# Chunked retention on one core: key moves, states and table loads in another order, and k ahead of q in its array

## What is computed

```python
x = hidden_states                       # (2, 512, 512)
xn = layernorm(x)
qkv = silu(xn @ qkv_w.T)                # 32 heads of 128: q, k, v
# retention, per head h with its own decay, carried over blocks of the sequence:
#   out = (q k^T * diag_decay) v + (q * q_decay) state
#   state = state * block_decay + (k * k_decay)^T v
attn = attn * rsqrt(mean(attn ** 2) + eps)          # over all heads
att_out = sigmoid(xn @ gate_w.T) * (norm_w * attn) @ out_w.T
# eight LoRA experts of rank 16, the two best of each token, and a base layer
ffn = xn @ W_base.T + b_base + expert_out
out = x + att_out + ffn
```

## Time and profile before

| | |
|---|---|
| three runs | 1157.47, 1155.29, 1155.59 us; median 1155.59 |
| the profiled execution | 1158.24 us |
| its span in the profile | 1156.4 us |
| TensorE busy | 1083.6 us, 94% of the span |
| ScalarE, VectorE, GpSimd busy | 59%, 57%, 55% |
| TensorE's granted clock, mean | 0.973 |
| share of TensorE in the chain that ended last | 66% |

### The profile page before, as it was taken

One profiled execution on the slowest core, in us unless ns is written; L12 is line 12 of the kernel. 1 busy time (PEld: TensorE's weight loads), 2 busy tenths in 40 slices (PEclk: granted clock), 3 DMA queues, 4 the chain that ended last, 5 costly groups with the idle time before them and its releaser, 6 DMA issues.

```text
span 1156.4 us, 20519 instructions
## 1 busy us (share of the span) xinstructions
PE 1083.6 (94%) x6258; PEld 948.4 (82%) x6258; DVE 655.3 (57%) x1212; ACT 679.7 (59%) x1465; POOL 634.0 (55%) x626
## 2 busy tenths in 40 slices
PE   9998999899998999989998999989999899989988
PEld 8987879788897878978897888978789688977777
DVE  6865564656554574655645555545646557454547
ACT  9665555565565565665656655555656556556521
POOL 6557463564635645475626746356464655357444
PEclk9998999999998999999999999989999999999899
DMA  8223122232213221131221312132211322223232
GB/s 301 56 60 101 43 64 56 56 83 51 60 46 97 65 69 51 33 90 54 68 55 55 82 47 59 49 86 73 68 56 32 86 59 68 55 56 82 62 89 89
DMA packets 150690, 81.28 MB, mean 70 GB/s; under 512 B 108896, under 2 KB 130656, under 8 KB 150624
## 3 DMA queue, kind: packets, MB, share of 16 engines
q1 hardware_dynamic: 150336, 80.04, 25.2%
q10 hardware_dynamic: 288, 0.52, 0.1%
HBM read 65.32 MB, written 15.20 MB: 70 GB/s over the span
## 4 chain that ended last, share of the span: by engine, by line
PE 66%; DMA 8%; DVE 8%; ACT 7%; issue 6%; SPq 4%; POOL 1%; ACTq 0%; DVEq 0%; POOLq 0%
PE bank_q L1907 6%; PE bank_q L1909 6%; PE bank_q L1908 6%; PE bank_p L1907 4%; PE bank_p L1908 4%; PE outp L1907 4%; PE bank_p L1909 4%; PE outp L1908 4%; PE outp L1909 4%; PE bank_r L1907 4%; DMA keys_t<-keys_dram 4%; PE bank_r L1908 4%; PE bank_r L1909 4%; DMA keys_dram<-k_blocks 3%; PE att L2007 2%
## 5 line engine op out<-in xcount | busy, mean ns | idle before, releaser
L459 POOL TENSOR_TENSOR w_lo<-combo,w_hi 128x768 fp32r<-128x768 f32 (+1 forms) x128 | 164.9, 1293 | 142.8 <-ACT w_hi L655 142.1
L459 POOL TENSOR_TENSOR w_lo<-raw,w_hi 128x256 fp32r<-128x256 f32 (+1 forms) x128 | 132.8, 1040 | 120.5 <-ACT w_hi L655 120.0
L510 POOL TENSOR_TENSOR sum_sq<-sum_sq,square 128x512 f32<-128x512 f32 x64 | 82.6, 1291 | 117.7 <-ACT square L825 117.7
L1471 DVE TENSOR_TENSOR acc<-acc,outp 128x512 f32<-128x512 f32 x116 | 79.3, 684 | 61.7 <-PE outp L1909 61.2
L1907 PE MATMUL outp<-wo_hi,g_hi 128*128 128x512 f32 x250 | 100.2, 401 | 13.4 <-DVE g_lo L1417 8.2
L1908 PE MATMUL bank_q<-c_lo,w_hi 128*128 128x512 f32 x276 | 108.3, 393 | 0.0
L1907 PE MATMUL bank_q<-c_hi,w_hi 128*128 128x512 f32 x276 | 108.3, 392 | 0.0
L1909 PE MATMUL bank_q<-c_hi,w_lo 128*128 128x512 f32 x276 | 108.2, 392 | 0.0
L1908 PE MATMUL outp<-wo_lo,g_hi 128*128 128x512 f32 x250 | 98.7, 395 | 0.0
L1909 PE MATMUL outp<-wo_hi,g_lo 128*128 128x512 f32 x250 | 98.4, 394 | 0.0
L1306 DVE TENSOR_TENSOR xs<-bank_r,xs 128x512 f32<-128x512 f32 x64 | 44.3, 691 | 94.9 <-ACT xs L655 75.3
(11 more groups left out here) (318 smaller groups left out, 3486.2 us busy)
## 6 DMA issues: line engine op xcount, KB each, us to landing
raw<-w_chunks SPq DMA_DIRECT2D x165, 256.0 KB, 3.3
keys_dram<-k_blocks SPq DMA_DIRECT2D x256, 32.0 KB, 1.6
keys_t<-keys_dram SPq DMA_DIRECT2D x128, 64.0 KB, 2.4
near_dram<-near SPq DMA_DIRECT2D x2, 2048.0 KB, 9.8
table<-near_dram SPq DMA_DIRECT2D x32, 128.0 KB, 2.0
fade<-near_dram SPq DMA_DIRECT2D x32, 128.0 KB, 3.6
y<-x SPq DMA_DIRECT2D x8, 256.0 KB, 4.3
out<-acc SPq DMA_DIRECT2D x7, 256.0 KB, 2.2
```

The costliest lines, as they stand in the source:

```text
L459: pool.tensor_tensor(piece(w_lo[i % 2], j), piece_source(i, j), piece(w_hi[i % 2], j).bitcast(F32), ALU.subtract).then_inc(wlo[j], 1)
L510: pool.tensor_tensor(sum_sq[:, s % 2, :], sum_sq[:, s % 2, :], square[:], ALU.add).then_inc(summed, 1)
L1471: dve.tensor_tensor(tile, tile, outp, ALU.add).then_inc(acc_done, 1)
```

## The change

Nothing is computed otherwise. These are the pieces; those in the loop body are made in the same way in the first and in the last group.

```diff
 # arrays that y[b] is laid over: k now first, q last
-                q_hi[b] = sb(f"q_hi{b}", [P, SEQ], F32R, within)
-                q_lo[b] = sb(f"q_lo{b}", [P, SEQ], F32R, within)
                 k_hi[b] = sb(f"k_hi{b}", [P, 2, P], F32R, within)
                 k_lo[b] = sb(f"k_lo{b}", [P, 2, P], F32R, within)
                 q_odd[b] = sb(f"q_odd{b}", [P, 2, P], at=within)
                 k_all[b] = sb(f"k_all{b}", [P, SEQ], at=within)
+                q_hi[b] = sb(f"q_hi{b}", [P, SEQ], F32R, within)
+                q_lo[b] = sb(f"q_lo{b}", [P, SEQ], F32R, within)
...
 # SyncE
                 load_rows(0, 20 * g + 8, 20 * g + 9)
+                move_keys(g, 2)
                 load_fade(4 * g + 1)
                 unit_taken(g, QK2)
                 load_rows(1, 20 * g + 13, 20 * g + 17)
-                move_keys(g, 2)
                 move_keys(g, 3)
...
                 move_keys(g, 4)
-                load_fade(4 * g + 2)
+                if not final:
+                    load_fade(4 * g + 2)
                 unit_taken(g, QK3)
                 if final:
...
                     sp.dma_start(raw[0][:, :, :].rearrange("p a n -> p (a n)"), hw_dram).then_inc(raw_in[0], 16)
+                    load_fade(4 * g + 2)
...
                 load_near(4 * g + 3)
+                load_fade(4 * g + 3)
                 move_keys(g, 6)
-                load_fade(4 * g + 3)
                 move_keys(g, 7)
...
-            for b in range(BATCH):
-                sp.wait_ge(cross_ready, STEPS * SGS - 1 + b)
-                for t in range(TB):
+            for u, b in ((0, 0), (0, 1), (1, 0), (1, 1)):
+                sp.wait_ge(scored if u == 0 else cross_ready, STEPS * SGS - 1 + b)
+                sp.wait_ge(k_turned, STEPS * SGS - 1 + b)
+                for t in (2 * u, 2 * u + 1):
                     sp.dma_start(y[b][:, t, :], x_tok[:, b * TB + t, :]).then_inc(y_in[b][t // 2], 16)
...
 # ScalarE
                 probs(0)
+                copy_u3(V1)
                 keys(0)
-                copy_u3(V1)
...
 # VectorE
                 lo(QK1, "p")
+                turn_keys(2)
                 lo(QK1, "q")
-                turn_keys(2)
...
                 probs_lo(2)
+                turn_keys(3)
                 add_out(-1)
                 gated_lo(1)
                 state_low(2)
-                turn_keys(3)
...
                 lo(QK3, "x")
+                turn_keys(6)
                 lo(QK3, "q")
-                turn_keys(6)
...
 # TensorE
                 output(-1)
+                prod(QK2, 2)
                 state(2)
-                prod(QK2, 2, 5)
-                prod(QK2, 7)
+                prod(QK2, 5, 7)
                 inter(2)
                 attend(2)
                 prod(QK2, 4)
-                scores(3)
+                scores(3, with_state=True)
                 prod(QK2, 3)
-                prod(G23, 1)
-                state(3)
+                prod(G23, 1, 6)
                 output(0)
-                prod(G23, 6)
                 prod(G23, 2)
...
                 prod(QK0, 2)
+                prod(QK0, 5)
                 state(6)
-                prod(QK0, 5, 7)
+                prod(QK0, 7)
+                prod(QK0, 4)
                 inter(6)
                 attend(6)
-                prod(QK0, 4)
                 scores(7)
```

## The result

The changed kernel takes 1163.45 us (median of 6 runs, 1162.13 to 1167.82), the kernel before 1156.3 us beside it (1154.81 to 1158.26): a ratio of 1.0071, 95% interval [1.0049, 1.0092]. It is 7 us slower. The profiled execution took 1163.12 us with a span of 1161.3, against 1158.24 and 1156.4, so the traces account for 4.9 us of it; the rest is that the profiled execution of before lay over its median.

A forecast was written before the change was run, and what follows sets the result against it. TensorE, busy 94% of the span, was taken to bound the kernel by its idle and low-clock time. Terms -17.6 + 25.8 + 3.2 + 4.5 - 5.8 + 4.2 - 1.0 = +13.3 us gave 1169 us, range 1150 to 1184.

The forecast's parts named there:

- Step 2: Around state(2), eight times: keys written ahead of fade and weight loads, a product moved into idle time; 2.2 us gained each.
- The first rival: At state(2): weights land sooner and the clock is kept, gain up to 4.1 us a group, 1149 to 1154 us; chance 0.18.
- Step 6: Around state(6), eight times: fade load ahead of keys 6 makes them late, output(8) starts later; +25.8, +3.2 and +4.5 us.
- The term of 4.3 a group: Groups 1 to 6: late keys 6 and new product order start output(8) at 571.1 instead of 566.79; 25.8 us lost.
- The term for the clock: Idle places at state(6), prod(QK0, 4) and output(8): one clock drop of 1.5 us in every second group, 4.5 us.
- Last group: Last group: earlier hw_dram fetch removes the stall at prod(G23, 3), -5.8 us; y's tiles load later, delaying output(8), +4.2.
- the fetch: Last group: hw_dram fetch ahead of the fade load ends 2.71 us idle and 3.1 of low clock, -5.8 us.
- The longer wait for y's tiles: End of last group: y[0]'s tiles 2 and 3 load later, output(8) at 1127.4 instead of 1121.45; +4.2 us, bounds 0 and 6.
- Rest: Remaining pieces: copy_u3(V1) ahead of keys(0) removes waits of 0.17 us, 1.0 in all; moved turn_keys(6) is hidden.
- the V1 copy: ScalarE: copy_u3(V1) ahead of keys(0) removes waits of 0.17 us, -1.0 us in all.

The follow-up runs named there:

- the kernel with the wait alone: Changed kernel with the fade load put back behind keys 6, but its wait for the cross product left ahead of them: 1153.40 us, ratio 0.9963.
- the kernel with step 6 alone: Kernel before plus the fade load ahead of keys 6, the earlier turn_keys(6) and the new product order around state(6): 1191.53 us, ratio 1.0303.

## Why the prediction was right

The sign, the range and every place named were right; the size was not. Between the two traces the segments sum to 4.8 us, where the forecast had 13.3.

- **Step 2**, forecast -17.6 us, between the traces -21.5, alone -20.5. The gain was 2.2 a group in the sum and measured 2.7 on the average (2.0 to 3.7). The steps hold: keys first, weights late next, 2.4 us idle forecast and 2.68 measured, `w_hi` the releaser. From fade issue to weights it took 5.21 us (496.28 to 501.49) and not the 5.07 of the row. Mis-sized was the low clock behind it, which I let stand in full. The idle time shrank by 1.9 us a group on the average (forecast 2.3), and 0.8 more came back behind it, from the clock. The forecast took group 3 for all groups, and in group 3 the clock gave nothing: over the 6.8 us behind `state(2)` it was 0.77 there before, but 0.56 in group 1, and 0.75 in both afterwards. Groups 1 and 3 before, then now:

```profile
227.50:234.30 6.80, 6.78 (x20) 5.55 (x21) 1.30 (x3) 3.99 (x7) 5.20 (x3) 0.56 0.09 22
500.00:506.80 6.80, 6.80 (x28) 5.79 (x29) 1.30 (x3) 4.45 (x8) 5.36 (x3) 0.77 0.08 19
...
225.70:232.50 6.80, 6.76 (x31) 5.77 (x32) 2.98 (x7) 5.46 (x12) 6.72 (x7) 0.75 0.20 39
503.00:509.80 6.80, 6.78 (x31) 5.79 (x32) 2.98 (x7) 5.28 (x11) 6.72 (x7) 0.75 0.20 39
```

- **The first rival** asked for weights that land sooner and a clock that is kept, and neither came in the changed kernel. The Trainium skill's figure in "DMA: Bandwidth & Descriptors", section "Anatomy of one DMA", stood on its side; that section fits it to DMAs that GpSimd issues, and these are SyncE's. The weights took 5.21 us where the estimate by it was 3.7. The fade load and the keys' read ahead are part of it: from their own issue the weights took 4.38 us here (497.11 to 501.49) and 3.38 without those two ahead. Which of the two it is was not tried.
- **Step 6**, forecast +33.5 us. The term of 4.3 a group was 4.2 to 4.4 in groups 2 to 6 (4.29 in group 3), and in group 3 every start came within 0.15 us, counted from `state(5)`; of the idle places only `prod(QK0, 4)` was off, 1.31 us and not 1.7. The wait for `fade_cross(5)` as its main cause is shown by the kernel with the wait alone. In group 0 `output(8)` came 3.0 us later (forecast 3.2), of which 1.0 came back behind it, since its own wait fell from 2.07 to 1.57 and the clock stayed up. The term for the clock, 4.5, went wrong in its place: three idle places of 1.3 to 1.75 us cost none, and some 4 us came in group 1, whose `state(6)` waited 3.36 us. In all +31.1; that group 1's loss nearly filled the place of the 4.5 is luck.
- **Group 1.** There SyncE wrote keys 6 at 277.48 and read them at 282.27, 4.8 us later and not 3.5. In six places of the five kernels with the wait for `fade_cross(5)` ahead of keys 6 this stretch took 4.4 to 4.8 us: in group 1 of each, and in group 0 of the kernel with step 6 alone. In just these six the profile has one packet of the instruction queue q8 (0.02 MB) in it; in the other 34 it took 3.8 us or less, and there was none. Below are the queues (packets, MB, share of the 16 engines) from the keys' write to their read in group 1 of the changed kernel. No run moved that packet, so that it is the cause is not shown.

```profile
q1 hardware_dynamic: 720, 0.26, 21.4%
q8 instruction: 1, 0.02, 1.2%
```

- **The fade load's transfer.** The forecast had put "the fade's own issue and a gap" for what stands ahead of the keys. It did not see that the transfer also slows the keys' own, 3.50 us from write to read and not 2.92. Issue and transfer together are 1.0 us of what the load costs a group.
- **Last group**: the fetch -5.4 for -5.8 between the traces. Alone it was worth 3.8; later waits took 0.6 back, and the rest is within the interval. The longer wait for y's tiles gave +3.8 for +4.2: counted from `state(5)`, `output(8)` came 4.8 us later (forecast 5.9), and 1.0 came back behind it (forecast 1.7). It began at 1127.35, where the forecast had 1127.4, but this is chance: the forecast counted on the time axis of the trace before, and this group's `state(5)` stood 1.1 us later on it.
- **Rest**: the V1 copy gave 3.2 us and not 1.0. That is more than its waits of 0.17; I priced the idle time at one place and not what ScalarE has behind the copy. Which of that it is was not tried.

The sum of what the traces show is -21.5 + 31.1 - 5.4 + 3.8 - 3.2 = +4.8. Of the 8.5 us too many, 3.9 are step 2's, 2.4 step 6's and 2.2 the V1 copy's. The pieces measured alone sum to -20.5 + 35.7 - 3.8 - 3.0 + 3.4 (the wait for y, from the traces) = +11.8, against 7.2 measured together; each has an interval of 1.4 to 2.3 us to either side, so nothing follows from the difference.

## What to carry to other kernels

SyncE issues its loads in order, so a load costs what it waits for, and all that stands behind it pays. The issue of the fade load takes 0.4 us, and in the kernel before its data was used 8 us after it (554.08 and 562.31). Ahead of the keys it cost 25 us in eight groups: 16 because its own semaphore came 3 us after the keys behind it were ready, and 9 because its issue and its transfer were then ahead of theirs. Ask of every moved issue which semaphore it waits for and when that comes. And look for stretches where the queue waits for a landing: the weights issued in one of these held the keys' read up by 0.2 us only. And when the wait for one thing goes, look on the same engine for the next that is late; here removing the first gave 20 us and removing the second 34 more.

## What the runs showed of the hardware

- The granted clock in the 3.4 us behind an idle place of TensorE, over the traces of all fourteen kernels: 1.00 after each of the more than 200 waits of 0.9 to 1.87 us, 0.72 or less after each of the more than 60 of 3.17 us or longer. From 1.92 to 3.14 us it went both ways, at the same place of neighbouring groups too: 0.57 after 1.92 and 1.00 after 2.08, 0.66 after 2.61 and 1.00 after 2.73, 1.00 even after 3.05 and 3.14.
- One long wait was therefore dearer than three short ones: 3.17 and 0.61 us, 3.8 together, in one kernel took the same time within what is measured as 1.72 + 1.31 + 1.74, 4.8 together, in the other.
- Two issues on one queue that look alike do not land alike: the same two transfers of 256 KB took 4.42 us behind a fade load and the keys' read, and 3.38 without. The keys' write took 2.92 us, 3.50 right behind a fade load, and 4.4 to 4.8 where an instruction packet moved meanwhile.
- Two kernels with the same instructions up to `state(7)` of the last group differed there by 4 us in the profiled executions, mostly in steps of 1.2 to 1.4 us behind `state(2)` or `state(6)`, where one had the lower clock longer, and by 2.9 us the other way in group 1.
